# Finer filler, moved weight rounding and a later store around the router of an attention and mixture-of-experts kernel

## The reference

```
h    = tanh(ctx @ Ws [77] + norm(x) @ W [1024] + b)       # every pair of token and row
att  = softmax(h @ w + mask);  t = att @ ctx
x    = x + tanh(t . Wcw + bcw) * norm(x) + tanh(t . Wcb + bcb)
```

```
probs = softmax(norm(x) @ gate);  score, idx = top_k(probs.T, k=512)      # per expert
y     = gelu(norm(x)[idx] @ W1[e] + b1[e]) @ W2[e] + b2[e]                # 256 -> 1024 -> 256
x     = x + sum_e scatter(idx, y * score) + gelu(norm(x) @ Ws1 + bs1) @ Ws2 + bs2
```

## Time and profile before

| | |
|---|---|
| median of 3 runs | 911.36 us (909.56 to 911.91) |
| profiled execution | 906.81 us |
| its span, first to last instruction | 905.1 us |
| busy: PE, DVE, ACT, POOL | 803.4, 712.6, 768.1, 312.5 us |
| TensorE's granted clock, mean | 0.984 |
| last tanh ends | near 620 us |
| total matmuls of the ten tests | 641.8 to 669.5 us |
| experts | from about 700 us |

### The profile page before, as it was taken

The page is one execution under the profiler, slowest core; times in us unless marked ns, Lnnn a source line. Parts: engine busy times, 40 slices in busy tenths (PEclk is TensorE's granted clock), DMA queues, the critical chain, the costliest instruction groups (busy, mean ns, idle before and its releaser), DMA issues.

```text
span 905.1 us, 14088 instructions
## 1 busy us (share of the span) xinstructions
PE 803.4 (89%) x5355; PEld 471.3 (52%) x5355; DVE 712.6 (79%) x1412; ACT 768.1 (85%) x600; POOL 312.5 (35%) x563
## 2 busy tenths in 40 slices
PE   6975678568999999899999999999877999999995
PEld 4321123114343444444544445546765899999985
DVE  5799888998979698988889895985787777667640
ACT  4989999999999999999999999996651677676671
POOL 3300540536524007674101820070303144454423
PEclk9899999999999999999999999999999999999998
DMA  8000000000001000200000110003102365545512
GB/s 266 15 1 1 1 1 1 1 24 23 2 1 47 1 1 24 70 1 1 24 1 1 34 38 1 24 24 105 36 1 73 119 183 140 141 118 113 136 21 34
DMA packets 32405, 41.80 MB, mean 46 GB/s; under 512 B 2365, under 2 KB 29011, under 8 KB 32339
## 3 DMA queue, kind: packets, MB, share of 16 engines
q1 hardware_dynamic: 26083, 32.49, 10.9%
q0 software_dynamic: 6144, 8.39, 5.6%
q10 hardware_dynamic: 112, 0.04, 0.0%
HBM read 28.33 MB, written 12.58 MB: 45 GB/s over the span
## 4 chain that ended last, share of the span: by engine, by line
PE 34%; ACT 29%; issue 7%; POOL 6%; DVE 5%; ACTq 0%; DVEq 0%; POOLq 0%
ACT z L975 24%; PE bank L894 10%; PE bank L917 9%; PE bank L774 4%; PE bank L825 4%; PE bank L810 2%; ACT u L1012 2%; POOL xn L1103 2%; ACT z L971 2%; PE bank L703 1%; PE bank L932 1%; DVE z L1333 1%; ACT L1012 1%; PE bank L868 1%; DVE onehot L1609 1%
## 5 line engine op out<-in xcount | busy, mean ns | idle before, releaser
L975 ACT ACTIVATE z<-z 128x4096 f32<-128x4096 f32 (+5 forms) x157 | 520.7, 3360 | 8.6 <-DVE z L1333 8.2
L1333 DVE TENSOR_SCALAR z<-feat,txt_bias 128x1024 f32<-128x1024 f32 (+1 forms) x722 | 422.8, 656 | 21.2 <-PE bank L774 19.9
L774 PE MATMUL bank<-z,window 128*32 128x512 f32 x2464 | 308.9, 606 | 64.0 <-ACT z L975 62.5
L774 PEld LDWEIGHTS bank<-z,window 128*32 128x32 f32 x2464 | 68.7, 110 | 247.4 <-issue 138.0
L825 PE MATMUL bank<-ws_sb,u 128*128 128x256 f32 x512 | 126.0, 388 | 0.0
L825 PEld LDWEIGHTS bank<-ws_sb,u 128*128 128x128 f32 x512 | 92.3, 190 | 39.1 <-issue 28.6
L810 PE MATMUL bank<-tr,ws_s 128*128 128x512 f32 x384 | 109.1, 422 | 0.5 <-issue 0.5
L894 PE MATMUL bank<-xg_s,w_s 128*128 128x512 f32 x384 | 99.5, 397 | 0.2 <-DVE xg_s L1635 0.2
L917 PEld LDWEIGHTS bank<-w_s,hid_s 128*128 128x128 f32 x672 | 86.3, 188 | 4.0
L810 PEld LDWEIGHTS bank<-tr,ws_s 128*128 128x128 f32 x384 | 71.1, 193 | 32.9 <-issue 19.6
L917 PE MATMUL bank<-w_s,hid_s 128*128 128x256 f32 x672 | 88.2, 280 | 0.0
(11 more groups left out here) (237 smaller groups left out, 783.3 us busy)
## 6 DMA issues: line engine op xcount, KB each, us to landing
w_raw<-in_L_ffn_W_dram SPq DMA_DIRECT2D x16, 1024.0 KB, 5.7
x_ring<-in_x_dram SPq DMA_DIRECT2D x8, 512.0 KB, 8.5
xn_dram<-xn SPq DMA_DIRECT2D x8, 512.0 KB, 2.9
out_dram<-x_ring SPq DMA_DIRECT2D x8, 512.0 KB, 2.9
u<-in_L_ffn_Ws_dram SPq DMA_DIRECT2D x1, 1024.0 KB, 11.2
ws_sb<-in_L_ffn_Ws_dram SPq DMA_DIRECT2D x1, 1024.0 KB, 13.6
xg<-xn_dram,idx POOLq DMA_INDIRECT x32, 4.1
out_dram<-y,idx POOLq DMA_INDIRECT x32, 3.9
```

The source lines that it names most:

```text
L774: ins = e.matmul(sums[v][32 * r:32 * r + 32, :], window[:, c, 31 - k:63 - k], z[:, n % ZB, at_piece:at_piece + TOK], start=(v, r) not in b ...
L975: e.activation(part, part, ACT.Tanh).then_inc(signal(*step), 1)
L1333: ins = e.tensor_scalar(z[:, n % ZB, i * width:(i + 1) * width], feat_of(units, c), bias_of(units, t, c), None, ALU.add)
```

## The change

The change touches the order only, and one wait of SP.

- A piece of filler is half an `up` (three matmuls) or a quarter of a `down` (one matmul) instead of a whole `up` and half a `down`. The numbers of pieces at each place are new.
- The eight roundings of the weights of expert 0 (`split_hi`, 128 x 512 each) leave the tests, one to a test, and stand beside masks, ranks, slots and the first list. The two roundings of y of unit 7 (`y_hi`) go to two tests instead of one.
- `listed` stands directly behind the last `list` of its expert, ahead of the filler there. `SECOND_FILL` has a zero behind the second list's first piece.
- `down_ends` of unit 7 leaves the end of the filler, which stood ahead of `listed` of expert 1, for slice 2 of expert 0 (`LAST_END`).
- The loads of W1 and W2 of expert 1 stand behind the turning of expert 0's rows, and the first of them also waits for the four gathers to land.

```
-ENDS_BEHIND = 3
+ENDS_BEHIND = 6
...
-TAIL_FILL = (4, 3)
+TAIL_FILL = (9, 6)
...
-TEST_FILL = (2, 4, 2, 2, 2, 2, 0, 4, 2, 0)
-RANK_FILL = (2, 2, 3, 2)
-EXPERT_FILL = (10, 5, 1)
-SECOND_FILL = (3, 1, 2, 2, 5)
-LIST_FILL = (1, 0, 0, 0)
+TEST_FILL = (4, 6, 4, 4, 3, 4, 3, 6, 4, 0)
+RANK_FILL = (4, 3, 5, 3)
+EXPERT_FILL = (23, 13, 0)
+SECOND_FILL = (7, 0, 3, 5, 7)
+LIST_FILL = (2, 1, 0, 0)
+LAST_END = 2
...
+    def up(v, m):
+        return [[("up", v, m, 0, passes // 2)], [("up", v, m, passes // 2, passes), ("gelu", v, m)]]
+    def down(v, m):
+        return [[("down", v, m, j, j + 1)] for j in range(J)]
...
-    filler = begun(va) + last_ffn[:ENDS_BEHIND] + [down_ends(va)] + last_ffn[ENDS_BEHIND:] + [down_ends(vb)]
+    filler += last_ffn[:ENDS_BEHIND] + [down_ends(va)] + last_ffn[ENDS_BEHIND:]
...
-    order += [("load_w1", 1), ("load_w2", 1)]
...
-    by_scalar = [[("y_hi", vb, c) for c in reversed(range(C))], *[[step] for step in first_split]]
+    by_scalar = [[("y_hi", vb, c)] for c in reversed(range(C))]
...
-        order += [("mark_slots", 0, q), ("list", 0, q)]
+        order += [("mark_slots", 0, q), ("list", 0, q), high.pop(0)]
+        if q == 3:
+            order.append(("listed", 0))
...
         order += [("mark_slots", 1, q), ("list", 1, q)]
+        if q == 3:
+            order.append(("listed", 1))
         fill(SECOND_FILL[1 + q])
-    order += [("listed", 1), ("fold", 1), ("folded", 1), ("gather", 1)]
+    order += [("fold", 1), ("folded", 1), ("gather", 1)]
...
+        if ex == 0 and m == LAST_END:
+            steps += down_ends(vb)
...
-    order += turn_gathered(0) + low[PIECES[0]:]
+    order += [*turn_gathered(0), *low[PIECES[0]:], ("load_w1", 1), ("load_w2", 1)]
...
+                    if ex == 1:
+                        for a in range(A):
+                            e.wait_ge(first_gathered[a], 16)
```

More of the change, by code:

```diff
@@ L207, in fill @@
                 order.extend(filler.pop(0))
[L209 to L220, removed]
-    lead = [step for steps in filler for step in steps]
[L223 to L233, removed]
-    filler = begun(va) + last_ffn[:ENDS_BEHIND] + [down_ends(va)] + last_ffn[ENDS_BEHIND:] + [down_ends(vb)]
+    def up(v, m):
+        return [[("up", v, m, 0, passes // 2)], [("up", v, m, passes // 2, passes), ("gelu", v, m)]]
+    def down(v, m):
+        return [[("down", v, m, j, j + 1)] for j in range(J)]
+    lead = [step for steps in filler for step in steps]
+    filler = [piece for m in range(4) for piece in up(va, m)] + down(va, 0) + down(va, 1) + up(va, 4) + up(va, 5)
+    for m in range(2, M):
+        filler += down(va, m) + (up(va, m + 4) if m + 4 < M else [])
+    last_ffn = up(vb, 0) + [piece for m in range(1, M) for piece in up(vb, m) + down(vb, m - 1)] + down(vb, M - 1)
+    filler += last_ffn[:ENDS_BEHIND] + [down_ends(va)] + last_ffn[ENDS_BEHIND:]
     def split(name, ex, h):
@@ L256, in work_order @@
     order += [step for step in lead if step[0] == "down" and step[1:3] not in late]
-    fill_chain(4)
+    fill_chain(8)
     ends = [step for step in lead if step[0] in BY_VECTOR]
@@ L286, in work_order @@
     order += end[13]
+    high, low = [*first_split], [("split_lo", *step[1:]) for step in first_split]
     fill(RANK_FILL[0])
-    order += [("masks",), ("ranks",), ("rank_total",)]
+    order += [("masks",), high.pop(0), ("ranks",), ("rank_total",)]
     fill(RANK_FILL[1])
-    order += [("offsets",), ("ranked",)]
+    order += [("offsets",), high.pop(0), ("ranked",)]
     order.append(("slots_turn",))
     fill(RANK_FILL[2])
-    order.append(("slots",))
+    order += [("slots",), high.pop(0)]
     order.append(("mark", 0))
@@ L296, in work_order @@
     for q in range(4):
-        order += [("mark_slots", 0, q), ("list", 0, q)]
+        order += [("mark_slots", 0, q), ("list", 0, q), high.pop(0)]
+        if q == 3:
+            order.append(("listed", 0))
         fill(LIST_FILL[q])
-    order += [("listed", 0), ("fold", 0), ("folded", 0), ("gather", 0)]
-    low = [("split_lo", *step[1:]) for step in first_split]
+    order += [*high, ("fold", 0), ("folded", 0), ("gather", 0)]
     order += low[:PIECES[0]]
```

## The result

The changed kernel took 911.08 us (909.04 to 912.90, 18 runs). The kernel before, beside it on the same chips, took 909.30 (905.76 to 911.91, 18 runs). The ratio is 1.0029, with a 95% interval of 1.0017 to 1.0040, so +2.6 us; the two medians themselves are 1.8 us apart. A second measurement of the same program gave 1.0017 (1.0001 to 1.0032), +1.5 us. The forecast was +1.05 us (912.4 against 911.36) and called anything within 0.3% no change. The measured loss lies at or under that size, but the intervals leave out zero: the change makes the kernel a little slower. Nearly half of the 4.55 us that the forecast put between the profiled run and the median was a draw of three; over 18 runs the median of before is 2.5 us above the profiled run.

The account below looks back on a forecast made before the run. TensorE was taken to bound the kernel, full in the experts but with holes ahead of them. The terms -3.0 + 3.85 + 0.2 = +1.05 us, put on the median 911.36, gave 912.4 us; range 908.0 to 915.7.

Parts of the forecast that it names:

- The tests, -2.0: Count, total, decide, ask loops ahead of the experts: finer filler and moved roundings end them 2.0 us earlier.
- test 0: Up to total 1: one rounding of y leaves ScalarE's path, saving 0.5 less 0.1, so -0.4 us.
- test 1: Took 4.11 us; with four quarters of down and the up instead of six, -0.8 us.
- total 6 to total 8: Late stretch of tests: 6.67 us becomes 5.9, with weight roundings gone but `down_end` still ahead of `decide` 7; -0.8.
- the third rival: Tests don't shorten: TensorE's clock falls there, the 2.0 us are lost, +3.0, 914.4 us; chance 0.08.
- The second list, -2.2 warm: Second list up to its fold, without clock cost: fold at 694.1 instead of 698.35, -4.2 us with the tests included.
- The clock there, 1.2: TensorE's clock falls again in the second list, costing 1.2 us, bounds 0 and 1.7.
- the whole start of the experts (-3.0): Experts start 3.0 us earlier: -4.2 at the second fold, less 1.2 for the clock.
- The store, +3.85: In the experts, unit 7's store behind a weight load lands at 729.2, making expert 1's first down 3.85 us late.
- my upper bound: Latest landing allowed for unit 7's store in the experts: 731.3, from 8.2 us behind a load.
- the second rival: Experts: load takes 7.3 us, store lands at 731.3, down 5.95 late, clock costs 1.4; +4.35, 915.7 us; chance 0.20.
- The rest of the hole: 4.45, and 0.2 for the clock: Experts: 4.45 us from W2's rounding to the remainder expert 1's first down needs, plus 0.2 for a clock drop.

Follow-up runs that it names:

- the late end alone: Kernel before, with only unit 7's `down_ends` moved from the end of the filler to slice 2 of expert 0: 913.72 us against 907.88, ratio 1.0071.
- after once more: The changed kernel run again, unaltered, against the kernel before: 909.74 us against 907.78, ratio 1.0017.
- the even second fill: Changed kernel with `down_ends` at slice 1 and `SECOND_FILL` (10, 2, 2, 2, 2) for (7, 0, 3, 5, 7): 898.72 us against 907.26 for before, ratio 0.9913.
- the run behind the load: Changed kernel, unit 7's store issued from ScalarE's queue, held until after the load of W1 of expert 2: 909.94 us against 908.27 for before, ratio 1.0022.
- the first experiment: Changed kernel with unit 7's `down_ends` at slice 1, so its store precedes the load on SP: 903.23 us against 907.88 for before, ratio 0.9945.

## Why the prediction was right, step by step

- *The tests, -2.0.* Measured where the clock held: -1.9 to -2.1 (25.80 and 25.68 against 27.73). In the two executions of after it was -1.35 and -1.15, because one test ran at half rate. Term by term, test 0 gave 0.2 to 0.3 (forecast 0.4), test 1 0.87 (0.8), and total 6 to total 8 came to 5.85 to 5.91 us (5.9) wherever the clock held there. The reason given for the last one was wrong in part: the roundings that left the tests cost nothing there with the new filler, as their return shows. That the clock may fall there was the third rival, given 0.08, and it cost 0.6 to 0.8 and not 2.0.
- *The second list, -2.2 warm.* Measured without a half-rate stretch: -1.7 (27.18 against 28.86). I had read the waits of TensorE right (first piece, one-hot, no wait for `picked`) and the sum came 0.5 short: from the second piece to the third and on to the fourth it took 2.25 and 2.58 us, where 2.0 and 2.2 had been summed. Nearly all of the gain is the half-rate stretch of before that is missing and the wait for `picked`, and both come with the late end alone (26.54).
- *The clock there, 1.2.* Nothing in one execution of after, 2.7 in the other (29.87 less 27.18), 1.5 in four others of the same second fill (28.65 to 28.69). As a mean of such draws 1.2 is fair; as the cost of one profile it isn't. In the profile of after the whole start of the experts (-3.0) came to -0.3.
- *The store, +3.85.* Place, wait and everyone queued behind it were as told: SP issued it 0.47 us behind the load, ScalarE waited ahead of the rounding of W2, TensorE for the gelu. The size was off. I let the store land 1.4 us behind the load, from the pair of the earlier trace rows; it landed 3.0 behind it, 8.2 after its issue. Its packets were through, but for one, 1.0 after the load's landing, near what I had taken; the last packet and its landing took 2.0 more, beside the gathers. All five late stores of the profiles have such a last packet, 0.6 to 1.4 us behind the others. The load itself took 5.7, as typical as I had assumed. Working forward from the earlier trace rows the sum would have been 722.6 + 5.7 + 3.0 = 731.3, which was my upper bound. The measured loss is 7.0, against the 5.95 + 1.4 of the second rival. So the hole was as long as in the rival *longer and cold*, and its clock fell, but that cost little (next point). The cause was not a load of 7.3 us, as given there; the gathers that the rival named did stand beside it, but at the store's last packet and not at the load. That they caused the delay of this packet is read from the order of the packets; no run without the gathers was made.
- *The rest of the hole: 4.45, and 0.2 for the clock.* The up behind the hole took 2.93 us instead of 1.45. Yet most of what the stage lost beyond the landing is not the clock. From the start of the rounding to the first down 5.28 us passed in after, and 5.13 in the run with the store on ScalarE's queue, whose granted clock was 1.00 all the way. The term of 4.45 is what it missed. It ended with VectorE's remainder of W2, which indeed took 4.5 us in both (728.38 to 732.89, 725.99 to 730.49); but there the remainder of the hidden slice (`e_lo`, 0.69 us) stood behind it, and the down followed this one within 0.1 us. In before it had run ahead, in VectorE's idle time. Against that warm run, to the end of the kernel, the clock behind the hole cost nothing to 0.3 us in after and the two other runs in which the stretch ended by the down or soon after it, and 1.1 to 1.2 in after once more and in before with the late end, where it was longer. So 0.2 was right for some executions, and the rival's 1.4 nearly right for others.
- *The sum.* By stages the second execution of after has -1.15 - 1.68 + 7.30 + 0.64 = +5.1 against the profile of before, and the medians +1.5 to +2.6. The difference lies ahead of the tests and in the baseline: the profiled run of before is 2.5 us under its median in the first comparison and 0.5 to 1.5 us under it in the later ones. Both profiles of after start their tests near 639.0; before starts at 641.76, before with the late end at 642.0, and the ten relatives of after at 639.9 to 642.9. So a part of the good agreement is luck: a stall too small by 3 us (2.3 of it the landing, 0.7 the `e_lo`) was set against a baseline that was 2 to 3 us too good. Whether the new fill ahead of the tests shortens that stage (the means say by 1 us, with a scatter of 4) stays open.

The Trainium skill (DMA: Bandwidth & Descriptors, Queues, rings and completion order) says that each engine takes the rows that have work in turn, packet by packet. The trace agrees for the time in which both had packets, with 191 against 189. The run behind the load adds what the rule doesn't cover: the store on a row of its own had no packet for its first 3 us, and the rounding began 8.4 us after its issue. The forecast used the same section for "the store waits out the load". The wait is there, but the order within one queue is not needed for it.

## What to carry to other kernels

A store or load that another engine will wait for should be issued ahead of a large transfer, not behind it. Best is well ahead, as in the first experiment. Another queue didn't help here, and 0.4 us of order was worth 3 us (35.20 against 38.18). Price it by the landing of the transfer ahead plus its own landing alone (here 5.7 + 2.9), and look at what else will run at its end. When a producer on VectorE feeds short pieces on TensorE, put filler of just the producer's length between all the pieces: a zero behind the first leaves a wait with work in hand. And a change that moves an end off one path should be checked for who waits for what that end releases.

## What the hardware showed that was not expected

- The landing of a store of 512 KB: 2.9 us alone; 5.8 issued 0.25 ahead of a load of 1 MB; 8.2 issued 0.47 behind it; a rounding 8.4 after issue when it stood 0.16 behind it on another queue.
- Two queues that both had work moved equal numbers of packets (191 and 189), not equal bytes (0.78 and 0.19 MB).
- TensorE's half rate is not fixed by the program. The same program showed 6.7 us of it in the second list in one execution and none in the other. Over 14 executions the even second fill had none there in three, the uneven lumps of after and its relatives had it in five of nine. That is too few to call the even fill the cause. In after TensorE had idled 1.82 us ahead of the first list piece before it fell and 0.89 us ahead of the second; the same two waits stood in an execution whose clock held (1.80 and 0.89, after once more).
- The time of an execution goes only loosely with its mean granted clock. Of the 79 of before in the experiments, 30 with 0.984 and more had a median of 906.8 us and 13 with 0.975 and less 910.1; between them there is no order (13 with 0.977 had 907.3, 7 with 0.981 had 909.5).
